# A four-layer graph network on one core: the own rows' half of the fourth phase's inner layer is formed in the third phase

## What is computed

```
h = jnp.maximum(_layernorm(x, axis=-1), 0.0)
x = x + _L2_gnn_ref(h, src, dst, ...)

def sage_conv(h, W_self, W_neigh, b):
    agg = jax.ops.segment_sum(h[src], dst, num_segments=N) / deg
    return h @ W_self + agg @ W_neigh + b
h = jax.nn.relu(sage_conv(x, W_self1, W_neigh1, b1))      # 128 -> 256
return sage_conv(h, W_self2, W_neigh2, b2)                # 256 -> 128
```

## Time and profile before

| | us |
|---|---|
| median of 3 runs | 5160.67 |
| lowest, highest | 5158.96, 5161.46 |
| the profiled execution | 5161.02 |
| its span | 5159.0 |
| PE, DVE, ACT, POOL busy in it | 4072.5, 3400.9, 2990.4, 3073.0 |

### The profile page before, as it was taken

How to read it: one execution, slowest core, us unless ns; L and a number is a source line. 1 busy time by engine, 2 the same in 40 slices (tenths; PEclk the granted TensorE clock), 3 DMA queues, 4 the chain that set the end, 5 groups by cost and what they waited for, 6 DMA issues and landing times. The chain is left out here.

```text
span 5159.0 us, 130637 instructions
## 1 busy us (share of the span) xinstructions
PE 4072.5 (79%) x23084; PEld 3055.8 (59%) x23085; DVE 3400.9 (66%) x12207; ACT 2990.4 (58%) x6766; POOL 3073.0 (60%) x3244
## 2 busy tenths in 40 slices
PE   6967775777689996766699999978888177777777
PEld 2334443777677775656577777767776155555555
DVE  9989995555478885777333333347777257777777
ACT  6835552666567775666454545546666155556555
POOL 0057772777577765777544444347664677777771
PEclk9989997999889997887799999999999589999998
DMA  1023331666556665887555555558877366666664
GB/s 23 0 62 102 104 103 60 197 212 198 175 167 199 199 198 173 261 256 245 167 178 177 174 180 176 172 180 270 268 266 257 102 180 199 202 201 197 198 198 143
DMA packets 599695, 905.37 MB, mean 175 GB/s; under 512 B 98488, under 2 KB 254280, under 8 KB 599600
## 3 DMA queue, kind: packets, MB, share of 16 engines
q1 hardware_dynamic: 467072, 670.37, 39.2%
q0 software_dynamic: 100352, 180.83, 14.3%
q10 hardware_dynamic: 32176, 53.17, 2.8%
HBM read 491.31 MB, written 412.69 MB: 175 GB/s over the span
## 5 line engine op out<-in xcount | busy, mean ns | idle before, releaser
L1020 PE MATMUL banks<-M,OH 128*128 x7840 | 1200.8, 311 | 383.4 <-POOLq L599 206.6
L570 POOL DMA_INDIRECT M<-table_a,six x1176 | 1125.4, 957 | 428.0 <-issue 324.5
L1020 PEld LDWEIGHTS banks<-M,OH 128*128 128x128 f32 x7840 | 1085.2, 213 | 431.4 <-issue 417.5
L570 POOL DMA_INDIRECT M<-table_b,six x784 | 767.1, 978 | 541.7 <-PE banks L1017 305.8
L659 ACT ACTIVATE AG<-banks x1176 | 632.3, 589 | 598.7 <-PE banks L1020 553.8
L565 POOL DMA_INDIRECT edges_by_block<-pack,pos_i x392 | 377.7, 964 | 417.2 <-DVE pos_i L1292 303.5
L677 ACT ACTIVATE HO<-H,BI,SC 128x128 f32 (+1 forms) x1176 | 484.0, 482 | 105.7 <-DVE BI L1453 58.6
L1406 DVE TENSOR_TENSOR OH<-banks,dstrel 128x1024 f32<-128x1024 f32 x392 | 478.8, 1222 | 85.5 <-PE banks L1020 72.2
L659 ACT ACTIVATE T<-banks 128x512 f32<-128x512 f32 (+1 forms) x588 | 294.7, 518 | 340.9 <-DMA table_a<-T 312.6
L570 POOL DMA_INDIRECT M<-table_pairs,dix x392 | 400.8, 1023 | 119.5 <-issue 100.0
L570 POOL DMA_INDIRECT M<-table_pairs,six x392 | 378.5, 966 | 128.2 <-issue 111.9
(11 more groups left out here) (313 smaller groups left out, 8321.2 us busy)
## 6 DMA issues: line engine op xcount, KB each, us to landing
XZ<-state SPq DMA_DIRECT2D x490, 256.0 KB
table_a<-T SPq DMA_DIRECT2D x294, 256.0 KB
state<-T SPq DMA_DIRECT2D x294, 256.0 KB
state<-H SPq DMA_DIRECT2D x196, 256.0 KB
h_turned<-HT ACTq DMA_DIRECT2D x196, 256.0 KB
table_pairs<-T SPq DMA_DIRECT2D x98, 512.0 KB
M<-messages SPq DMA_DIRECT2D x98, 512.0 KB
XZ<-in_x SPq DMA_DIRECT2D x194, 256.0 KB
```

Source lines behind the costliest of these rows:

```text
L570: nc.gpsimd.indirect_dma_start(out=M[:, slot, :], out_offset=None, in_=table, in_offset=bass.IndirectOffsetOnAxis(ap=idx, axis=0)).then_in ...
L1020: last = mm(banks[:, ds(sums_at[k], P)], OH[:, b * US + k, :], source[:, ds(rows_at[k], P)], start=False, stop=False, skip_group_check=True)
```

## The change

In the third phase PE gets a part `own3` (lag 6): it multiplies the transposed rows in `HT` by `ws1`, into `ps[5]` and `ps[6]`. ACT copies the first bank (`own_first`, lag 7), DVE the second (`own_second`, lag 7), and SP stores both, 512 KB for a group, to `own_products` (`store_own`). The transposed rows themselves are no longer stored. In the fourth phase SP loads both halves (`load_own`), into `Z` and into a new buffer `SX` that also holds two older weights, PE's `hidden4` forms the neighbours' half alone, DVE adds the stored half (`hidden_sums`, lag 4) into `H`, and ACT takes the relu in place.

```
@@ sync, third phase @@
             staggered(sp, [(3, placed(3, tabs[1], HO, (s_ho, "ho"), st)), (0, loaded(3, states[2], XB, (s_row, "row"), in_)),
-                           (2, whole_rows(3, states[3], H, (s_var, "var"), sv))])
+                           (2, whole_rows(3, states[3], H, (s_var, "var"), sv)), (6, store_own)])
+            def store_own(i, b):
+                g = 2 * i + b
+                sp.wait_ge(s_oa, g + 1)
+                sp.wait_ge(s_ob, g + 1)
+                sp.dma_start(own_d[g], both(b)).then_inc(sh[b], 16)
@@ sync, fourth phase @@
-            staggered(sp, [(0, scales4), (0, loaded(4, h3_d, Z, (s_mma, "mma"), in_)), (3, loaded(4, states[3], XB, (s_t2, "t2"), late)),
+            staggered(sp, [(0, scales4), (1, load_own), (3, loaded(4, states[3], XB, (s_t2, "t2"), late)),
+            def load_own(i, b):
+                g = 2 * i + b
+                need(sp, s_as, g - 1)
+                sp.dma_start(Z[:, b, :], own_d[g][:, 0:W4]).then_inc(in_[b], 16)
+                sp.dma_start(SX[:, b, :], own_d[g][:, W4:2 * W4]).then_inc(in_[b], 16)
@@ scalar @@
+            def own_first(i, b):
+                g = 2 * i + b
+                act.wait_ge(s_own, g + 1)
+                need(act, sh[b], turns(3, "sh", i))
+                copy(T12[:, b, 0, :], ps[5]).then_inc(s_oa, 1)
-            staggered(act, [(1, sums(2)), (3, deviations(3, (s_pre, at(3, "pre")))), (5, turned(3)), (3, normed(3, None)), (5, turned_stored(3, h3_d))])
+            staggered(act, [(1, sums(2)), (3, deviations(3, (s_pre, at(3, "pre")))), (5, turned(3)), (3, normed(3, None)), (7, own_first)])
             def hidden4(i, b):
-                act.wait_ge(s_mma, g + (at(4, "mma") + 1))
-                need(act, s_mm, g + (at(4, "mm") - 1))
-                nc.scalar.activation(H[:, b, 0, :], ps[5], ACT.Relu, bias=b1col[:, 0:1])
-                nc.scalar.activation(H[:, b, 1, :], ps[6], ACT.Relu, bias=b1col[:, 1:2]).then_inc(s_hid, 1)
+                act.wait_ge(s_as, g + 1)
+                nc.scalar.activation(H[:, b, 0, :], H[:, b, 0, :], ACT.Relu, bias=b1col[:, 0:1])
+                nc.scalar.activation(H[:, b, 1, :], H[:, b, 1, :], ACT.Relu, bias=b1col[:, 1:2]).then_inc(s_hid, 1)
@@ tensor @@
-            staggered(pe, [(0, walk(2)), (4, turn_rows(3, HO))])
+            def own3(i, b):
+                g = 2 * i + b
+                pe.wait_ge(s_ht, g + (at(3, "ht") + 1))
+                need(pe, s_oa, g)
+                need(pe, s_ob, g)
+                for h in range(2):
+                    last = mm(ps[5 + h], ws1[:, h * P:(h + 1) * P], HT[:, b, :], start=True, stop=True)
+                last.then_inc(s_own, 1)
+            staggered(pe, [(0, walk(2)), (4, turn_rows(3, HO)), (6, own3)])
             def hidden4(i, b):
-                pe.wait_ge(in_[b], turns(4, "in", i) + 16)
-                need(pe, s_hid, g + at(4, "hid"))
+                need(pe, s_as, g)
                 for h in range(2):
-                    mm(ps[5 + h], ws1[:, h * P:(h + 1) * P], Z[:, b, :], start=True, stop=False)
-                    last = mm(ps[5 + h], wn1[:, h * P:(h + 1) * P], HT[:, b, :], start=False, stop=True)
+                    last = mm(ps[5 + h], wn1[:, h * P:(h + 1) * P], HT[:, b, :], start=True, stop=True)
@@ vector @@
+            def own_second(i, b):
+                g = 2 * i + b
+                dve.wait_ge(s_own, g + 1)
+                need(dve, sh[b], turns(3, "sh", i))
+                v.tensor_copy(T12[:, b, 1, :], ps[6]).then_inc(s_ob, 1)
+            def hidden_sums(i, b):
+                g = 2 * i + b
+                dve.wait_ge(in_[b], turns(4, "in", i) + 32)
+                dve.wait_ge(s_mma, g + (at(4, "mma") + 1))
+                need(dve, s_mm, g + (at(4, "mm") - 1))
+                v.tensor_tensor(H[:, b, 0, :], ps[5], Z[:, b, :], ALU.add)
+                v.tensor_tensor(H[:, b, 1, :], ps[6], SX[:, b, :], ALU.add).then_inc(s_as, 1)
-            staggered(dve, [(4, summed_rows), (4, stats), (4, variances), (0, onehots(2)), (4, roots), (4, offsets)], chain, 2)
+            staggered(dve, [(4, summed_rows), (4, stats), (4, variances), (0, onehots(2)), (4, roots), (4, offsets), (7, own_second)], chain, 2)
-            staggered(dve, [(0, onehots(3)), (6, added(4, ...)), (2, pre4), (5, based4)], chain, 1)
+            staggered(dve, [(0, onehots(3)), (4, hidden_sums), (6, added(4, ...)), (2, pre4), (5, based4)], chain, 1)
```

More of the change, by code:

```diff
@@ L144, in program @@
         states = {d: dram(f"state{d}", [GROUPS, P, W4]) for d in (1, 2, 3, 4, 5)}
-        h3_d = dram("h3_turned", [GROUPS, P, W4])
+        own_d = dram("own_products", [GROUPS, P, 2 * W4])
         h5_d = dram("h5_turned", [GROUPS, P, W4])
@@ L180, in program @@
         dix = [sb(f"dix{k}", [P, 8 * GC], I32) for k in range(2)]
-        w1 = sb("w1", [P, P]); w2 = sb("w2", [P, P]); wlT = sb("wlT", [P, 2, P])
+        SX = sb("SX", [P, 2, W4]); w2, b2bc = (SX[:, 0, k * P:(k + 1) * P] for k in range(2)); wlT = sb("wlT", [P, 2, P])
         w31 = sb("w31", [P, 2, 2 * P])
@@ L190, in program @@
         wm = sb("wm", [P, P]); cm = sb("cm", [1, P])
-        b2bc = sb("b2bc", [P, P]); gam = sb("gam", [P, P]); bet = sb("bet", [P, P]); lbbc = sb("lbbc", [P, P])
+        gam = sb("gam", [P, P]); bet = sb("bet", [P, P])
         sb2bc = sb("sb2bc", [P, P]); be1bc = sb("be1bc", [P, P]); bu2bc = sb("bu2bc", [P, P])
@@ L286, in program @@
                "row": [0, 0, 1, 1, 0, 1, 0], "mma": [0, 0, 0, 0, 1, 0, 1], "hid": [0, 0, 0, 0, 1, 0, 1]}
-        TURN = {"in": [16, 16, 16, 16, 16, 16, 32], "late": [0, 0, 0, 0, 16, 0, 16], "st": [16] * 7,
+        TURN = {"in": [16, 16, 16, 16, 32, 16, 32], "late": [0, 0, 0, 0, 16, 0, 16], "st": [16] * 7,
                 "sv": [0, 16, 16, 16, 16, 16, 0], "sh": [0, 0, 0, 16, 0, 16, 0]}
@@ L458, in _ @@
             kept(2, "sv", sv)
+            def store_own(i, b):
+                g = 2 * i + b
+                sp.wait_ge(s_oa, g + 1)
+                stand(sp)
+                sp.wait_ge(s_ob, g + 1)
+                stand(sp)
+                sp.dma_start(own_d[g], both(b)).then_inc(sh[b], 16)
+            def load_own(i, b):
+                g = 2 * i + b
+                need(sp, s_as, g - 1)
+                stand(sp)
+                sp.dma_start(Z[:, b, :], own_d[g][:, 0:W4]).then_inc(in_[b], 16)
+                sp.dma_start(SX[:, b, :], own_d[g][:, W4:2 * W4]).then_inc(in_[b], 16)
             staggered(sp, [(3, placed(3, tabs[1], HO, (s_ho, "ho"), st)), (0, loaded(3, states[2], XB, (s_row, "row"), in_)),
-                           (2, whole_rows(3, states[3], H, (s_var, "var"), sv))])
+                           (2, whole_rows(3, states[3], H, (s_var, "var"), sv)), (6, store_own)])
             def placed5(i, b):
@@ L699, in do @@
                         need(act, s_mm, g + (at(d, "mm") - 1))
-                    if d in (3, 5):
+                    if d == 3:
+                        need(act, s_own, g - 1)
+                    if d == 5:
                         need(act, sh[b], turns(d, "sh", i))
@@ L1511, in based4 @@
                 link(v.tensor_tensor(q(XB[:, b, :]), q(XB[:, b, :]), four(sb2bc), ALU.add))
-            staggered(dve, [(0, onehots(3)), (6, added(4, lambda i, b: [q(XB[:, b, :])[:, 2 * h:2 * h + 2, :] for h in range(2)], sv, "sv")), (2, pre4), (5, based4)], chain, 1)
+            staggered(dve, [(0, onehots(3)), (4, hidden_sums), (6, added(4, lambda i, b: [q(XB[:, b, :])[:, 2 * h:2 * h + 2, :] for h in range(2)], sv, "sv")), (2, pre4), (5, based4)], chain, 1)
             settled(dve, 4)
```

7 lines of the change are left out of this document (5 added, 2 removed).

## The result

| | before, us | changed, us |
|---|---|---|
| median | 5161.07 | 5847.27 |
| lowest, highest | 5158.96, 5166.88 | 5843.75, 5853.3 |
| span of the profiled execution | 5159.0 | 5851.5 |

The ratio is 1.1333, with a 95% interval of 1.1318 to 1.1347. The forecast was 5745 us in 5610 to 5890, so the sign and the range held, and the size was short by 102 us.

A forecast was written before the change was run, and what follows sets the result against it. The kernel before was taken as bound by POOL's gathers in the third phase and by a full PE in the fourth. Adding +501 us for the third and +83 for the fourth to 5161 gave 5745 us, range 5610 to 5890.

The forecast's parts named there:

- Both loops: Third and fourth phases: engines wait for one another each turn, 10.3 us against 5.13 and 9.8 against 8.92.
- The signs asked for: Changed profile: DVE idle some 5 us before its copy, PE before own product and outer layer (2.3), DMA near 0.5.
- The loop's parts: Third phase's turn: DVE 4.14 us, ACT with handover 2.5, product with handovers and DVE's copy 2.8 to 4.5.
- The clock in the third phase: Own product takes 1.87 us at full clock, about 3.6 at half; the middle was taken, 10.3 us a turn.
- rival (a): Third phase: lower clock in every turn, loop 11.1 us, 5825 us in all; chance 0.20.
- the tail: Third phase's end: four turns without one-hots, 24 us, and four with only products and copies, 7 us.
- The clock in the fourth phase: Stops of over 2 us lower PE's clock now and then, 0.29 us a turn, 9.8 us against 9.55 without.
- What was costed at nothing: Fourth phase's ACT relu and larger loads cost nothing; phases 0 to 2, 5 and 6 unchanged.
- (b): Higher clock throughout: third phase 9.4 us a turn, fourth 9.55, 5640 us in all; chance 0.12.
- (d): Neither loop closed: PE full in fourth phase at 7.2 us, third at 5.88, 5067 us in all; chance 0.03.
- (c): Third phase's loop has missed slack and goes at the fifth's pace, 74 us more, 5318 us in all; chance 0.05.

The follow-up runs named there:

- the fillers: Changed kernel with six more 128x128 matmuls ahead of each group's transposes in the third phase; 6996.17 us, ratio 1.0747 to the kernel before.
- the sums first: Changed kernel with the fourth phase's sums that empty the outer layer's banks put ahead of the stored half's additions; 6796.89 us, ratio 1.0442.
- lag 8: Changed kernel with DVE's copy of the second bank made one turn later in the third phase; 6675.77 us, ratio 1.0254 on the first chip it ran on.

## Why the prediction was right, and where it was short

**Both loops: right.** The third phase was to be held by offsets, norming and copy, own product, DVE's copy; the fourth by two additions ahead of the sums that empty the outer layer's banks. Both show as forecast, in the chain of one turn and in the waits, and moving one part in each list took each away (on the other chips, where the changed kernel's phases are as long as on the first). The signs asked for were there: DVE idle ahead of its copy (6.2 us, forecast 5), PE idle ahead of the own product (2.2 us, ended by ACT's copy in 32 of 63 turns and under the name of "issue" in the others), PE idle ahead of the outer layer with DVE's sums as its end (2.25, forecast 2.37), POOL waiting for PE, and DMA at 0.42 and not at 0.98.

**The loop's parts: right to 0.15 us each.** Scaled rows to offsets 4.13 (4.14). ACT with its handover 2.46 (2.5). The rest beside the product 0.97 (0.91). The steps between engines were 0.34, 0.10 and 0.25, where 0.2, 0.12 and 0.12 had been taken from the earlier trace rows; the 0.34 holds the wait for the transposes, a branch that the prediction did not have.

**The clock in the third phase: the term that was mis-sized.** The step was to take the middle between 1.87 and 3.6 us for the own product, 10.3 us a turn. Of the 62 products in 2150 to 2850 us, 52 took 3.57 to 3.78 us and 10 took 1.95 to 2.54, so the turn was 11.2, slightly above rival (a)'s 11.1. The window's mean clock of 0.75 in place of the 0.81 of the earlier trace rows says the same. 50 of the 62 lie above 3.6 us, and the prediction had named a length outside 1.9 to 3.6 as the sign that its clock term is wrong. It was, by the choice of the middle, and by a little in the bound: a product wholly at the lower level takes 3.78. This is (11.2 - 10.3) x 91 = 82 us; the tail was 13 us in place of 31, and the phase +565 in place of +501.

The rule of the Trainium skill that is named beside rival (a) ("TensorE: Matmul & The Clock Gate", the part on the HAM clock gate), that the throttled level is the default and activity releases it, fits the product, and does not by itself tell which of a turn's two stops costs the level. The transposes follow a stop too, of 1.3 to 3.0 us in each turn, and 56 of 63 groups of four took 0.63 to 0.75 us, the higher level, and 7 took 1.00 to 1.12. The granted clock (the third number from the end) in one turn, during the transposes, from their end to the product, and during the product:

```profile
2418.41:2419.04 0.63, 0.63 (x4) 0.39 (x4) 0.23 (x2) 0.04 (x1) 0.33 (x2) 1.00 0.86 309
2419.04:2421.17 2.13, 0.00 (x1) 0.00 (x0) 0.00 (x0) 2.13 (x6) 1.56 (x2) 0.75 0.34 95
2421.17:2424.95 3.78, 3.78 (x6) 1.52 (x6) 0.00 (x0) 0.92 (x2) 0.00 (x0) 0.50 0.58 225
```

**The clock in the fourth phase: right in kind, short in size.** Without loss 9.69 us, forecast 9.55: the stop, which in the forecast's 2.37 held 0.16 for the end of the inner layer, was 2.25 + 0.17 = 2.42 by the same count, and the outer layer took 3.55 from start to start and not 3.46. The clock's part is (5.41 - 3.72) / 3 = 0.56 and was taken as 0.29, from the fifth phase's 0.96; the mean was 0.94. Together 10.25 in place of 9.8, 0.45 x 94 = 42 us, of the 44 that the phase was off.

**What was costed at nothing: right.** ACT's relu of a group ends at 3507.43, and the outer layer that reads it starts at 3516.38, a turn later. The larger loads don't show among the waits of the fourth phase. Phases 0 to 2, 5 and 6 together differ by under 1 us between the two spans.

**The rivals.** (a) was the case for the third phase, 565 us where it had 91 x 6.0 + 35 = 581. (b) is what the fillers went towards. The full PE of (d) in the fourth phase is what the sums first give (7.2 to 7.5 us a turn). The third phase near the fifth's 5.9 us, of (c) and (d), was not reached by any order on these chips, where it takes 6.6 and the kernel before about the same. Rival (d) put its condition as whether a product is done when DVE comes to its copy, and that is what lag 8 provides.

## What to carry to other kernels

When a step is split over phases or engines, the bytes and the matmuls are the small part of its price; ask of each new part which wait it carries and what is queued behind it on its engine. A part that empties a bank which the next matmul needs goes ahead of a part that waits for a matmul just issued, and a copy of a product belongs in a turn in which that product is already done: here these two places in two lists were worth some 10% of the kernel, and decided between 2% faster and 9% slower on the chips on which both were run. If a stop of some 2 us remains inside a loop, the matmuls behind it should be priced at both levels, with the lower one as a full case and not as half of one: here 52 of 62 products ran at it wholly or nearly so, one outer layer in three in part, and 7 of 63 groups of transposes.

## What the hardware showed that was not expected

- **Which stop costs the higher level.** Two stops of about the same length in one turn (2.14 and 2.29 us): behind the first the transposes run at the higher level (56 of 63 groups), behind the second the product runs at the lower (52 of 62). The granted clock falls between the two more often than anywhere else, and why is open. In the fourth phase one outer layer in three drops, in a strict rhythm, behind stops that are equal to 0.01 us.
- **More work on PE, less time.** Six extra matmuls a turn, 2.3 us of PE, took about 1% off the time (1.0747 and 1.0865 of the kernel before, on two chips).
- **Chips of the same kind, 26% apart.** The kernel before takes 5161 us on the chip of the first result and 6502 to 6568 on the four others. The operations last the same: the median gather is 944 ns on both. What is added are waits which the profile marks as "remote", and of which the first chip's trace of before has none. In the trace of before on one of the others, the three largest:

```profile
ACT AG L659 <- remote: 1002.4, 165, 81.3
DVE XZ L1534 <- remote: 520.7, 37, 19.9
ACT HT L659 <- remote: 484.1, 117, 12.4
```

  A stretch held by a loop through the engines takes the same on both (own products 1060 and 1058 us), and one that goes by gathers and loads does not (the third phase of before, 528 and 647). What is remote there, and why, no run here settles. For the ratio it means that the loss was 13% on one chip and 9% on another, from the same loop.
